# Reordering the five row groups inside a pair of column panels, and the vector work that follows them

## What is computed

```
h   = relu(layernorm(x))                         # 5120 x 64
e   = concat(c_u * (diag_u * h_u) @ W_u + h_u,   # rows 0..2047
             c_i * (diag_i * h_i) @ W_i + h_i)   # rows 2048..5119
t   = adj.T @ e                                  # the first product
g   = adj @ t                                    # the second product
out = x + layernorm(g) * gamma + beta + h
```

## Time and profile before

| what | value |
|---|---|
| median of three runs | 371.7 us |
| the profiled execution | 371.32 us, of which the span of the program is 369.5 us |
| PE busy | 360.3 us, 98% of the span |
| DVE busy | 263.0 us, 71% |
| POOL busy | 159.6 us, 43% |
| ACT busy | 74.3 us, 20% |
| moved by DMA | 133.22 MB, mean 361 GB/s |

### The profile page before, as it was taken

How to read it: one execution, slowest core, us unless ns; L and a number is a source line. 1 busy time by engine, 2 the same in 40 slices (tenths; PEclk the granted TensorE clock), 3 DMA queues, 4 the chain that set the end, 5 groups by cost and what they waited for, 6 DMA issues and landing times.

```text
span 369.5 us, 10865 instructions
## 1 busy us (share of the span) xinstructions
PE 360.3 (98%) x4776; PEld 151.7 (41%) x4776; DVE 263.0 (71%) x282; ACT 74.3 (20%) x213; POOL 159.6 (43%) x94
## 2 busy tenths in 40 slices
PE   7998999999999999999999999999999999999994
PEld 4664454543323443443334334334433343344432
DVE  5999994999061969395677839694956768385266
ACT  5863022010050004001300500040023005002422
POOL 2023060020019902970793199049607931990036
PEclk9999999999999999999999999999999999999998
DMA  8999999999999978989898989889898989853933
GB/s 311 422 419 415 418 426 419 419 419 402 403 380 411 363 291 331 427 343 411 323 429 331 419 326 425 338 318 421 349 409 326 427 339 413 325 247 132 426 130 142
DMA packets 19897, 133.22 MB, mean 361 GB/s; under 512 B 2209, under 2 KB 2977, under 8 KB 4001
## 3 DMA queue, kind: packets, MB, share of 16 engines
q1 hardware_dynamic: 19440, 132.22, 88.1%
q10 hardware_dynamic: 432, 0.66, 0.5%
HBM read 131.55 MB, written 1.31 MB: 360 GB/s over the span
## 4 chain that ended last, share of the span: by engine, by line
PE 87%; DMA 7%; POOL 2%; SPq 2%; DVE 1%; issue 0%; ACT 0%; DVEq 0%; POOLq 0%
PE h_acc L887 36%; PE t_acc L918 24%; DMA natural<-adj_rows 7%; PE x_acc L955 7%; PE h_acc L975 7%; PE t_acc L856 5%; PE t_acc L955 5%; PE h_acc L870 2%; POOL xs L424 1%; SPq L289 1%; POOL sums L420 1%; PE t_acc L993 1%; DVE xs L795 0%; SPq L286 0%; DVE sums L784 0%
## 5 line engine op out<-in xcount | busy, mean ns | idle before, releaser
L599 DVE STREAM_TRANSPOSE strips<-natural 128x2048 f32<-128x2048 f32 x76 | 169.0, 2279 | 48.2 <-PE h_acc L887 48.0
L887 PE MATMUL h_acc<-strips,tokens 32*64 32x512 f32 x2432 | 133.5, 589 | 0.1
L918 PE MATMUL t_acc<-natural,e 128*32 128x512 f32 x832 | 92.3, 592 | 0.1
L887 PEld LDWEIGHTS h_acc<-strips,tokens 32*64 32x64 f32 x2432 | 53.3, 132 | 79.4 <-issue 74.3
L399 POOL TENSOR_TENSOR sums<-natural 128x1024 f32<-128x1024 f32 x14 | 33.3, 2381 | 113.4 <-DMA natural<-adj_rows 113.4
L918 PEld LDWEIGHTS t_acc<-natural,e 128*32 128x32 f32 x832 | 27.4, 110 | 59.4 <-issue 58.2
L955 PE MATMUL x_acc<-sums,forms 128*32 128x256 f32 x280 | 41.1, 380 | 0.0
L856 PE MATMUL t_acc<-natural,e 128*64 128x256 f32 x320 | 36.5, 382 | 1.4 <-DMA natural<-adj_rows 1.1
L489 ACT COPY smalls<-x_acc 32x256 f32<-32x256 f32 x7 | 2.6, 365 | 170.1 <-PE t_acc L955 170.1
L479 ACT COPY tokens<-tokens 32x384 f32<-32x384 f32 (+2 forms) x60 | 24.2, 403 | 51.6 <-DVE tokens L623 30.9
L407 POOL TENSOR_TENSOR sums<-natural,sums 128x1024 f32<-128x1024 f32 x14 | 33.3, 2379 | 1.1
(11 more groups left out here) (97 smaller groups left out, 299.8 us busy)
## 6 DMA issues: line engine op xcount, KB each, us to landing
natural<-adj_rows SPq DMA_DIRECT2D x100, 1024.0 KB, 7.9
cols<-adj_cols SPq DMA_DIRECT2D x20, 1024.0 KB, 11.6
natural<-adj_last SPq DMA_DIRECT2D x4, 1024.0 KB, 10.8
out<-xs SPq DMA_DIRECT2D x4, 256.0 KB, 2.0
xs<-x ACTq DMA_DIRECT2D x2, 256.0 KB, 5.3
xs<-x SPq DMA_DIRECT2D x2, 256.0 KB, 7.7
out<-xs SPq DMA_DIRECT2D x2, 128.0 KB, 2.0
smalls<-small SPq DMA_DIRECT2D x1, 150.0 KB, 3.6
```

The lines of the kernel that those rows point to most:

```text
L599: nc.vector.transpose(strips[:, a, :, m].rearrange("p c t i -> p t c i"), natural[:, a, m].rearrange("p t (c j) -> p t c j", j=Q)).then_in ...
L887: last = nc.tensor.matmul(h_acc[D * s:D * (s + 1), q], t[part, a, b, u, :], rows, start=(isinstance(g, int) and g == 0 and b == 0 and u == 0),
L918: last = nc.tensor.matmul(t_acc[lane, pair_bank(half)].rearrange("p (a w) -> p a w", a=2), e[:, GT * m + 2 * k + s, Q * v:Q * (v + 1)], na ...
```

## The change

The order of the groups in a pair becomes 0, 4, 3, 1, 2 (it was 0, 1, 4, 2, 3). `first_early` does groups 0 and 4, `first_rest` groups 3, 1 and 2. Since group 4 of the pair after next now writes `x_acc` before the strips, PE waits there until DVE has read all of the pair before (`s_t_left`). PE's wait for `s_forms` stands ahead of `first_early(3)` instead of behind it. ACT copies `sixth` to `uv` after group 3, and DVE forms u and v from it ahead of `sum_pair`. DVE turns in the order 0, 3, 1, 2, and one turn is behind t instead of two; in pair 2 all eight turns come ahead of t. The loads are issued in an order of their own, with group 2 of an odd panel put behind group 4 of the next pair.

```diff
-ORDER = (0, 1, 4, 2, 3)
-EARLY = 2
-TURNS = (0, 1, 3, 2)
-BEHIND = 2
+ORDER = (0, 4, 3, 1, 2)
+TURNS = (0, 3, 1, 2)
+BEHIND = 1
@@ sync: loads
             for g in range(2, PAIRED + 2):
-                for m in range(GROUPS):
+                for m in range(GROUPS) if g < PAIRED else ORDER:
                     refill(g, m)
...
             for g in range(PAIRED + 2, PANELS, 2):
                 for a in range(2):
-                    for m in range(EARLY):
-                        refill(g + a, m)
-                for m in (4, 3, 2):
-                    for a in range(2):
-                        refill(g + a, m)
+                    refill(g + a, 4)
+                if g > PAIRED + 2:
+                    refill(g - 1, 2)
+                    refill(g, 0)
+                    refill(g, 3)
+                    refill(g + 1, 0)
+                    refill(g + 1, 3)
+                else:
+                    for m in (0, 3):
+                        for a in range(2):
+                            refill(g + a, m)
+                for a in range(2):
+                    refill(g + a, 1)
+                refill(g, 2)
                 for a in range(2):
                     refill_cols(g - 2 + a)
+            refill(LAST, 2)
             refill_cols(LAST - 1)
@@ scalar: pair
+                act.wait_ge(s_first, firsts_pair(half, 3))
+                nc.scalar.copy(uv, sixth).then_inc(s_sixth, 1)
                 act.wait_ge(s_first, firsts_pair(half, ORDER[-1]))
-                nc.scalar.copy(uv, sixth).then_inc(s_sixth, 1)
@@ vector: keep_t_pair
                 nc.vector.tensor_tensor(u, first_v, uv, ALU.add).then_inc(s_u, 1)
+                dve.wait_ge(s_u, 2 * (half - FIRST_HALF))
+                nc.vector.tensor_tensor(uv, seventh, uv, ALU.add).then_inc(s_v, 1)
+                dve.wait_ge(s_v, 2 * (half - FIRST_HALF) - 1)
+                nc.vector.tensor_tensor(v, first_v, uv, ALU.add).then_inc(s_v, 1)
                 sum_pair(half)
...
-                nc.vector.tensor_tensor(uv, seventh, uv, ALU.add).then_inc(s_v, 1)
                 dve.wait_ge(s_t_left, left + 3)
                 turn_t(2 * half, 0, slice(0, WIDE))
-                dve.wait_ge(s_v, 2 * (half - FIRST_HALF) - 1)
-                nc.vector.tensor_tensor(v, first_v, uv, ALU.add).then_inc(s_v, 1)
@@ vector: pair 2
-            turn_pair(FIRST_HALF, keep_t_plain)
+            for a in range(2):
+                for m in TURNS:
+                    turn_strips(PAIRED + a, a, FIRST_HALF, m)
+            keep_t_plain(FIRST_HALF)
@@ tensor
             def first_rest(half):
+                first_summed(half, 3)
+                for m in (1, 2):
+                    first_plain(half, m)
+
+            def first_early(half):
+                first_plain(half, 0)
+                if not isinstance(half, int):
+                    pe.wait_ge(s_t_left, LEFT * (half - FIRST_HALF - 1))
                 first_summed(half, 4)
-                first_plain(half, 2)
-                first_summed(half, 3)
-
-            def first_early(half):
-                for m in range(EARLY):
-                    first_plain(half, m)
...
+            pe.wait_ge(s_forms, 4 * len(SUMMED))
             first_early(FIRST_HALF + 1)
-            pe.wait_ge(s_forms, 4 * len(SUMMED))
```

More of the change, by code:

```diff
@@ L658, in keep_t_pair @@
                                         ALU.add).then_inc(s_t_left, 1)
-                dve.wait_ge(s_u, 2 * (half - FIRST_HALF))
                 dve.wait_ge(s_t_left, left + 2)
                 nc.vector.tensor_tensor(high[0], u, high[0], ALU.add).then_inc(s_t_left, 1)
-                nc.vector.tensor_tensor(uv, seventh, uv, ALU.add).then_inc(s_v, 1)
                 dve.wait_ge(s_t_left, left + 3)
                 turn_t(2 * half, 0, slice(0, WIDE))
-                dve.wait_ge(s_v, 2 * (half - FIRST_HALF) - 1)
-                nc.vector.tensor_tensor(v, first_v, uv, ALU.add).then_inc(s_v, 1)
                 dve.wait_ge(s_v, 2 * (half - FIRST_HALF))
```

## The result

| | kernel before | changed kernel |
|---|---|---|
| median of 17 runs each | 371.39 us | 372.79 us |
| lowest run | 371.26 us | 372.20 us |
| the profiled execution | 371.32 us, span 369.5 | 373.51 us, span 371.7 |
| ratio to before | | 1.0035, 95% interval 1.0021 to 1.0049 |

The change makes the kernel 0.35% slower. The forecast was 372.8 us, range 371.1 to 375.0.

What follows compares the result with a forecast made beforehand. PE, busy 98% of the span at full clock, was taken to bound the kernel. Terms -0.25 + 0.25 + 1.4 - 0.3 = +1.1 us took the median from 371.7 to 372.8, range 371.1 to 375.0.

Steps and rivals of the forecast that it cites:

- The loop, costed at nothing: Six turns of the pair loop, 33.84 us each: the new order neither gains nor loses, 0 for each turn.
- PE's arrival at `s_t_left`: In the loop, PE reaches its new wait at 210.25, DVE's additions end at 208.3: 1.9 us to spare.
- L613 0.6 earlier: Sign in the loop: DVE's addition L613 comes 0.6 us earlier after the last step.
- Rival C: In the loop, DVE's additions for t are held up behind POOL operations: +4.1 us, 375.8; chance 12%.
- Pair 2, -0.25: PE's plain steps of pair 2: the wait for load (5,4) goes, gaining 0.25 us.
- p0's wait, +0.25: Way into pair 3: p0 waits 0.25 us for load (7,0), landing at 105.3.
- The stall, +1.4: Before s4 of pair 3, PE waits 1.4 us for POOL's sums, ready at 110.1; bounds 1.3 to 1.9.
- The rule that said otherwise: The skill's fit: 4.4 us for a 1 MiB load, so a stall about 0.4 us shorter, sum +0.7.
- The end, -0.3: Before the last strips, the wait for t of panel 18 goes because t comes earlier, gaining 0.3 us.
- The sum: Whole kernel: -0.25 + 0.25 + 1.4 - 0.3 = +1.1 us, median 372.8.
- Rivals B and D: B: no stall before s4 of pair 3, 371.15, 13%. D: changes of shape cost less, 370.5 to 372.1, 5%.
- E: Rival at the last pair: t isn't earlier, the 0.3 at the end stays, +1.4 us, 373.1; chance 8%.

Runs made afterwards that it cites:

- the experiment with five additions: Five more DVE additions in the chain of t of pairs 3 to 8, against the changed kernel with group 4 ahead in pair 2: median 375.88 us.
- the experiment with the loads alone: Kernel before with only the loads of panels 4 and 5 in the order PE wants them (0, 1, 4, 2, 3): median 370.99 us, ratio 0.9988.
- group 4 first: Changed kernel with group 4 ahead of group 0 in pair 2 alone (loads, centring of e, plain steps): median 370.58 us, ratio 0.9977.

## Why the prediction was right

*The loop, costed at nothing.* Right: 33.83 in both. The three places where I had it tight held: PE's arrival at `s_t_left` (1.9 to spare by the prediction, 1.7 in the trace after, 1.5 by the experiment with five additions), DVE ahead of t (0.2; it waited 0.37), and the loads. The 1.9 was a little too much because the sign "L613 0.6 earlier" came out at 0.37: that addition starts 1.07 behind `loaded_pair` (207.08 against 206.01), where it was 1.44 and I had 0.87. Rival C needed a delay of more than that. The last two additions for t did come to lie beside POOL's operations, as it supposed, and kept their length. The timelines of DVE, of PE (s4, 1.67 behind the last addition) and of POOL in the changed kernel:

```profile
210.32 0.43 DVE L678 TENSOR_TENSOR t_sum<-x_acc,t_sum 32x256 f32<-32x256 f32 x1
210.78 0.43 DVE L679 TENSOR_TENSOR t_sum<-x_acc,t_sum 32x256 f32<-32x256 f32 x1
```

```profile
212.88 0.38 PE L968 MATMUL x_acc<-natural,e 128*32 128x256 f32 x1
```

```profile
210.48 2.38 POOL L408 TENSOR_TENSOR sums<-natural 128x1024 f32<-128x1024 f32 x1 [7.71 <-DMA natural<-adj_rows]
```

0.43 as before, the second with POOL at work all the while. The Trainium skill (SBUF — State Buffer, section Who interferes with whom) says that a VectorE instruction with at most one SBUF input, outside the 2-port modes, does not contend with GpSimd; the trace agrees.

*Pair 2, -0.25.* -0.36 in starts of steps, of which 0.07 is an earlier start of pair 2; 0.3 by the experiment with the loads alone.

*p0's wait, +0.25.* 0.43. The load (7,0), issued at 94.3, landed 10.8 later at 105.1 where I had 105.3; what I had left out is that p0 starts only 0.25 behind that landing.

*The stall, +1.4.* 1.33, with all of its links: issue 92.9 (I had 93.0), landing 100.2 (100.3), POOL's start 100.38 (100.5), PE's start 110.12 (110.1). The bounds 1.3 to 1.9 held at their lower end. The experiments show that it is this chain and not something beside it: issue the loads a step earlier and the time falls by what s4 gains, lengthen POOL's part and all of it is paid, with the lost clock on top.

*The rule that said otherwise.* The loads took 4.8 and 6.9 from issue, as in the rows of before, and not the 4.4 that is estimated from the Trainium skill's fit (DMA: Bandwidth & Descriptors, section Anatomy of one DMA — SWDGE (gpsimd) path); that fit is for DMAs issued by GpSimd, which these are not. The stall is as long as the rows made it.

*The end, -0.3.* 0.40, and it comes from u and v being formed early.

*The sum.* +1.1. The lowest runs differ by 0.94, the profiled executions by 2.19, or 0.95 without the 1.24 of the second loss, the medians by 1.40. What I did not foresee is in that last number: the changed kernel has more runs that lie a further 1 us up. The forecast number hit the median partly by luck, because I took the median before as 371.7 of three runs, 0.3 above that of 17, and this made up for what was missing. Rivals B and D did not happen, E neither (t was earlier and the wait at the end went).

*The second loss.* The profiles show loads of instructions, 16 KB each, as a DMA queue of their own (q8). In the two profiles with long strips of pair 2 (the changed kernel with 15.16, and the one with u and v late with 14.89) such a load starts at about 113.7, some 0.4 us after PE has begun those strips. The changed kernel's DMA queues from 108 to 113.6 and from 113.6 to 115 (queue, kind: packets, MB, share):

```profile
q1 hardware_dynamic: 320, 2.36, 101.1%
```

```profile
q1 hardware_dynamic: 84, 0.57, 98.9%
q8 instruction: 1, 0.02, 4.9%
```

and the same kernel in its second profile, from 108 to 113:

```profile
q1 hardware_dynamic: 287, 2.10, 100.7%
q8 instruction: 1, 0.02, 1.4%
```

There the load comes at 109.5, during PE's wait, and the strips take 13.91. In the other nine profiles the same load also comes ahead of the strips (105.4 in the kernel before, 107.5 with group 4 first, 116.2 with POOL's first addition twice, where the strips start at 118.59), and they take 13.92. But more such loads follow while the strips run, in the kernel before at 117.8 and 123.0, and nothing is lost with them. So what goes with the long strips is not an instruction load during them but this one load coming just behind their start; PE's "issue" at 116.27, an idle time that waits for nothing the profile shows, fits that. That the one causes the other is not shown: it rests on two profiles with and ten without, and what makes the load start earlier or later was not found.

Four runs of the changed kernel, at 374.3 to 375.5, are further up still. None was profiled, and the mean granted clock doesn't settle what they lost: it is 0.991 in two of them, as low as in the experiments where PE ran at half clock behind a wait (0.989 to 0.993), but 0.997 and 0.993 in the other two, and a run of the kernel before at 371.35 has 0.991 as well. The cause of these stays open.

## What to carry to other kernels

Where one engine is busy 98% of the time and the loop has no gap, a new order has nothing to gain in the loop, and it can lose outside it, as here on the way in: look at the first use of every operand that was moved earlier, follow it back through the helper engine to the load and to the event that frees its buffer, and add that chain up from rows of the same events. If it is late, move the first step that frees the buffer, not the loop: here one swap in the first pair took 1.6 us off the lowest run and 2.2 off the median. And price a long wait of the busy engine at more than its length: the two waits of 3.6 and 3.8 us here cost another 1.7 and 2.5 us of lost clock.

## What the runs showed of the hardware that I had not expected

Waits of 3.62 and 3.76 us on PE came with several us at half the granted clock: 1.7 us more for a step of 3.43 behind the first, 2.5 us more for a step of 3.16 behind the second. Waits of 0.53 and 1.12 us, in the profiles taken, did not. The Trainium skill (TensorE: Matmul & The Clock Gate, section Part 1: The HAM clock gate (the "warmup" mystery)) has just these two levels, 1.2 and 2.4 GHz; granted clocks of 0.55 and 0.72 over some 6 us, with 1.00 in the stretch behind each, agree with that.

Two profiles of one and the same kernel have an instruction load at 109.5 and at 113.7, and 13.9 and 15.2 us for the same 256 matmuls, at a full granted clock in both.
